# Fused four-layer kernel on one core: W's last part transposed earlier into another bank, a tanh layer's second half in quarters, two more tiles seeded by ScalarE

## The reference, cut to what matters

```python
x = x + diffusion(x, zX, zY, zR)                       # 5-point stencil with reflecting edges, + reaction term
# layer 1: scores of each row, softmax of them under a mask per row, pooling of the rows of x
attn_in = jnp.tanh(jnp.einsum('bsd,da->bsa', hidden, W1) + b1)      # W1: 512 x 128
scores = jnp.einsum('bsa,a->bs', attn_in, v)
p = jax.nn.softmax(jnp.where(mask, scores[:, None, :], NEG_INF), axis=-1)
x = x + jnp.einsum('bjl,bld->bjd', p, hidden) / cnt[..., None]
# layer 2: a 512 x 512 weight and bias chosen per batch
x = x + jnp.einsum('bnh,boh->bno', x, W) + b[:, None, :]
# layer 3: adapter 512 -> 128 -> 512, then layer norm; weights chosen per batch
z = jax.nn.relu(jnp.einsum('bsh,bhk->bsk', hidden, Wd) + bd)
y = hidden + jnp.einsum('bsk,bkh->bsh', z, Wu) + bu
x = x + (y - mu) * jax.lax.rsqrt(var + EPS) * g + b
```

## Time and profile before

| What | Value |
|---|---|
| Median of 3 runs | 583.63 us (580.74 to 593.93) |
| The profiled execution, whole | 589.26 us |
| Its span, first to last instruction | 587.4 us |
| Mean granted TensorE clock | 0.975 |
| TensorE matmul row busy | 561.6 us (96%) |
| TensorE weight loads | 440.1 us (75%) |
| VectorE | 447.8 us (76%) |
| ScalarE | 335.8 us (57%) |
| GpSimd | 291.7 us (50%) |
| DMA | 93.84 MB, mean 160 GB/s |

### The profile page before, as it was taken

How to read it: one execution, slowest core, us unless ns; L and a number is a source line. 1 busy time by engine, 2 the same in 40 slices (tenths; PEclk the granted TensorE clock), 3 DMA queues, 4 the chain that set the end, 5 groups by cost and what they waited for, 6 DMA issues and landing times.

```text
span 587.4 us, 9333 instructions
## 1 busy us (share of the span) xinstructions
PE 561.6 (96%) x2934; PEld 440.1 (75%) x2934; DVE 447.8 (76%) x1176; ACT 335.8 (57%) x587; POOL 291.7 (50%) x271
## 2 busy tenths in 40 slices
PE   8996689999999999999999999999999999999995
PEld 2356577788768887788768887788769887788784
DVE  7745778778975988778975988778976988767456
ACT  3434465466846667466846567465846568445440
POOL 6635441577328553577228553577237653326221
PEclk9696979999999999999999999999999999999999
DMA  5479008795499548994499548994599548124352
GB/s 167 138 273 162 2 1 259 238 186 103 115 302 239 110 85 229 309 199 93 122 300 236 114 89 199 335 201 82 129 278 251 118 94 196 21 72 80 76 98 88
DMA packets 60000, 93.84 MB, mean 160 GB/s; under 512 B 10999, under 2 KB 15607, under 8 KB 59952
## 3 DMA queue, kind: packets, MB, share of 16 engines
q0 software_dynamic: 16544, 29.90, 31.0%
q1 hardware_dynamic: 34192, 46.58, 24.8%
q10 hardware_dynamic: 9216, 16.78, 7.8%
HBM read 61.26 MB, written 31.98 MB: 159 GB/s over the span
## 4 chain that ended last, share of the span: by engine, by line
PE 85%; DVE 8%; issue 3%; ACT 2%; DMA 1%; POOL 0%; SPq 0%; DVEq 0%; ACTq 0%
PE y L644 34%; PE front_ps L680 9%; PE front_ps L644 8%; PE front_ps L758 6%; PE front_ps L703 5%; PE front_ps L656 4%; DVE x2f L1456 4%; PE front_ps L723 3%; PE front_ps L688 3%; PE y L813 2%; PE front_ps L694 2%; PE y L669 2%; PE y L665 2%; PE front_ps L733 1%; DVE xd L1321 1%
## 5 line engine op out<-in xcount | busy, mean ns | idle before, releaser
L534 POOL TENSOR_TENSOR norm<-norm 128x1 f32<-128x1 f32 x64 | 45.1, 704 | 134.1 <-DVE norm L1489 134.1
L644 PE MATMUL y<-wth,x2h 128*128 128x512 f32 x256 | 102.7, 401 | 0.0
L644 PE MATMUL y<-wth,x2l 128*128 128x512 f32 x256 | 100.6, 393 | 0.0
L644 PE MATMUL y<-wtl,x2h 128*128 128x512 f32 x256 | 100.0, 391 | 0.0
L541 POOL DMA_DIRECT2D out<-o_sb x58 | 64.7, 1154 | 39.2 <-ACT o_sb L1060 38.2
L1478 DVE BATCH_NORM_STATS2 stats<-y 128x6 f32<-128x512 f32 x64 | 44.4, 693 | 50.0 <-PE y L644 50.0
L510 POOL TENSOR_TENSOR xd<-xn 128x1024 f32<-128x1024 f32 x28 | 54.2, 1937 | 43.6 <-DVE x L1328 23.0
L558 POOL TENSOR_TENSOR x2l<-x2f,x2h 128x1024 fp32r<-128x1024 f32 x24 | 57.4, 2390 | 29.7 <-ACT x2h L929 29.7
L1456 DVE SCALAR_TENSOR_TENSOR x2f<-alb,small,front_ps 128x128 f32<-128x128 f32 x256 | 70.1, 340 | 1.2
L758 PEld LDWEIGHTS front_ps<-th_pt,x 128*128 128x128 f32 x512 | 62.8, 194 | 9.1 <-DVE x2f L1456 6.8
L758 PE MATMUL front_ps<-th_pt,x 128*128 128x129 f32 x512 | 65.5, 281 | 3.2 <-DVE x2f L1456 2.7
(11 more groups left out here) (149 smaller groups left out, 1176.5 us busy)
## 6 DMA issues: line engine op xcount, KB each, us to landing
xn<-in_x SPq DMA_DIRECT2D x32, 512.0 KB, 10.2
out<-x ACTq DMA_DIRECT2D x58, 256.0 KB, 4.7
out<-o_sb POOLq DMA_DIRECT2D x58, 256.0 KB, 6.2
xu<-in_x SPq DMA_DIRECT2D x21, 512.0 KB, 9.7
xu<-in_x POOLq DMA_DIRECT2D x21, 512.0 KB, 7.8
wn<-in_L_cond_weight SPq DMA_DIRECT2D x8, 1024.0 KB, 5.7
wd<-in_L_cond_down_w SPq DMA_DIRECT2D x8, 256.0 KB, 6.0
wu<-in_L_cond_up_w SPq DMA_DIRECT2D x8, 256.0 KB, 3.8
```

Source lines behind the costliest of these rows:

```text
L534: pool.tensor_tensor(rstd[:, r:r + 1], ve[:, r:r + 1], minus_half[:, :], ALU.pow).then_inc(rstd_ready, 1)
L644: ins = mm(dst, lhs, rhs, start=first and q == 0, stop=last and q == len(parts) - 1, skip_group_check=True)
```

## The change

W's last part goes to cbank, right behind adapter_down, instead of to pair_a behind spread_bias; what guards it is rest_w of part 1. The hidden layer's second half becomes two quarters: rows 512 to 767 in cbank, rows 768 to 1023 in pair_a, each with a tanh of its own. Tiles 1 and 7 join those seeded by ScalarE. ScalarE's and VectorE's orders follow.

```diff
@@ banks, constants
-        hidden_ps = (cbank, pair_a[:, 0:512])
+        HIDDEN = (slice(0, HALF), slice(HALF, HALF + 2 * P), slice(HALF + 2 * P, S))
+        hidden_ps = (cbank, cbank[:, 0:2 * P], pair_a[:, 0:2 * P])
-        w_ps = (pair_b, cbank, pair_a[:, 0:D])
+        w_ps = (pair_b, cbank, cbank)
-        SEEDED = (3, 4, 5, 6)
+        SEEDED = (1, 3, 4, 5, 6, 7)
@@ TensorE: transpose_x1, the waits for c = 0 to 3
-                wait_past(pe, *((wtl_ready, 3 * n - 2), (wtl_ready, 3 * n), (x1t_ready, NC * n + 1),
+                wait_past(pe, *((wtl_ready, 3 * n - 2), (zf_ready, 4 * n), (x1t_ready, NC * n + 1),
                                 (x1t_ready, NC * n + 2))[c])
@@ TensorE: score_hidden
-            def score_hidden(n, q, h):
-                pe.wait_ge(x1t_ready, NC * n + 2 * h + 2)
-                if h == 0:
+            def score_hidden(n, q, part):
+                pe.wait_ge(x1t_ready, NC * n + part + 2)
+                if part == 0:
                     wait_past(pe, x2s, KD * NG * n)
-                    wait_past(pe, wtl_ready, 3 * n - 1)
+                    wait_past(pe, wtl_ready, 3 * n)
+                elif part == 1:
+                    pe.wait_ge(th_ready, 3 * n + 1)
                 for k in range(KD):
-                    ins = mm(hidden_ps[h], w1[:, k, :], x1t[q][:, k, half(h)],
+                    ins = mm(hidden_ps[part], w1[:, k, :], x1t[q][:, k, HIDDEN[part]],
                              start=k == 0, stop=k == KD - 1)
@@ TensorE: spread_scores
-                pe.wait_ge(th_ready, 2 * n + h + 1)
                 pe.wait_ge(x1t_ready, NC * n + 3)
-                mm(pair_b[:, half(h)], v_col[:, 0:1].to_broadcast([P, P]), th[:, half(h)], start=True, stop=True
-                   ).then_inc(sc_ps, 1)
+                for part in ((0,), (1, 2))[h]:
+                    pe.wait_ge(th_ready, 3 * n + part + 1)
+                    ins = mm(pair_b[:, HIDDEN[part]], v_col[:, 0:1].to_broadcast([P, P]), th[:, HIDDEN[part]],
+                             start=True, stop=True)
+                ins.then_inc(sc_ps, 1)
@@ TensorE: scores_by_row, down_through_w
-                pe.wait_ge(th_ready, 2 * n + 2)
+                pe.wait_ge(th_ready, 3 * n + 3)
@@ TensorE: transpose_w
                     if hb == 3:
-                        pe.wait_ge(zf_ready, 4 * n + 4)
+                        pe.wait_ge(wtl_ready, 3 * n + 2)
@@ TensorE: linear
-                if t < 2 or t == 7:
+                if t == 0:
@@ TensorE: program, the opening
                     score_hidden(m, 1 - q, 1)
+                    score_hidden(m, 1 - q, 2)
@@ TensorE: program
                     adapter_down(n, q)
+                    transpose_w(n, 2)
...
                     spread_bias(n, q)
-                    transpose_w(n, 2)
                     linear(n, q, 0)
...
                     score_hidden(m, 1 - q, 1)
                     spread_scores(m, 0)
+                    score_hidden(m, 1 - q, 2)
                     spread_scores(m, 1)
@@ ScalarE: hidden(n, part) works on HIDDEN[part]; seed
+                act.wait_ge(bias_kept, b + 1)
                 act.wait_ge(y_free, NJ * b + before(t, YB) + 1 + CREDIT)
@@ ScalarE: program, the last tiles of the last batch
                     store_last(2)
-                    for t in range(5, NJ):
+                    keep_last_x3(5)
+                    seed(b, 7)
+                    store_last(3)
+                    for t in range(6, NJ):
@@ ScalarE: program, the opening
                     hidden(m, 1)
+                    hidden(m, 2)
@@ ScalarE: program
                     round_x2(n, q, 2)
                 if b is not None:
+                    seed(b, 7)
                     scale(b, 4)
...
                     adapter_relu(n, 0)
+                    round_w(n, 2)
                     adapter_relu(n, 1)
                     keep_x1t(m, 1 - q, 0)
-                    round_w(n, 2)
-                    scale(b, 5)
+                    keep_bias(n)
                     scale_rows(m, 3)
+                    seed(n, 1)
                     centre(m, 2)
                     keep_x1t(m, 1 - q, 1)
                     centre(m, 3)
+                    scale(b, 5)
                     scale(b, 6)
-                    keep_bias(n)
                     keep_x3(n, 0)
...
                     keep_x1t(m, 1 - q, 3)
+                    hidden(m, 1)
+                    hidden(m, 2)
                     round_up(m, 1 - q)
-                    hidden(m, 1)
@@ VectorE: program
                     diffuse(m, 1 - q, 1)
+                if n is not None:
+                    rest_w(n, 2)
                 if b is not None:
                     moments(b, 7)
                     subtract_mean(b, 1 - q, 7)
-                if n is not None:
-                    rest_w(n, 2)
```

More of the change, by code:

```diff
@@ L970, in keep_x1t, with hidden @@
                      pair[:, :].rearrange("p (k q) -> p k q", k=KD)).then_inc(x1t_ready, 1)
-            def hidden(n, h):
+            def hidden(n, part):
                 wait_past(act, p_mm, KD * n)
-                act.wait_ge(h_ps, 2 * n + h + 1)
-                act.activation(th[:, half(h)], hidden_ps[h], ACT.Tanh,
+                act.wait_ge(h_ps, 3 * n + part + 1)
+                act.activation(th[:, HIDDEN[part]], hidden_ps[part], ACT.Tanh,
                                bias=b1_col[:, 0:1]).then_inc(th_ready, 1)
@@ L1180, in program @@
                 if n is not None:
-                    round_w(n, 2)
-                if b is not None:
-                    scale(b, 5)
+                    keep_bias(n)
                 if m is not None:
                     scale_rows(m, 3)
+                if n is not None:
+                    seed(n, 1)
+                if m is not None:
                     centre(m, 2)
```

## The result

The changed kernel took 581.22 us in the median of 20 runs (576.72 to 590.15), against 585.85 us for the kernel before (20 runs, 580.74 to 594.05). The ratio is 0.9924, with a 95% interval of 0.9896 to 0.9953: faster by 0.8%, some 4.5 us, where 7.9 us (1.4%) were forecast. The time lies in the range; the gain is a little over half of the forecast, and against the 583.63 us from which the forecast started the 581.22 us are only 2.4 less.

A forecast was written before the change was run, and what follows sets the result against it. TensorE's instruction stream was taken to set the period. The terms, -5.8 - 1.3 - 1.7 + 0.8 + 1.5 - 1.4 = -7.9 us, taken from 583.63, gave 575.7 us, with a range of 570 to 584.

The forecast's parts named there:

- 1, W's last part: Transposes of W's last part no longer wait for pair_a: 0.57 us a middle batch, 5.8 us in all.
- 2, the two seeds: Linear of tiles 1 and 7 loses a bias matmul, 0.233 us each: 1.7 us for tile 1, 1.3 for tile 7.
- less 0.2: Tile 1's seed in the first batch: 0.2 us taken off the 0.233 us won in each of 8 batches.
- That is a tie: Tile 7's seed seen at 272.25, linear reaching it at 272.21: 0.15 us gained in each of 7 batches.
- 3, the quarters: Tanh layer's second half in two 256-column parts: 0.8 us added for ten more passes a batch, 1.5 for the stall.
- The stall becomes 0.24 - 0.21 + 0.43 = 0.46, so 0.22 is lost in each of 7 batches: TensorE's wait on the last tanh in spread_scores, with less cover: 1.5 us added in all.
- 4, the opening: First batch's hidden layer no longer waits whole for keep_x1t(3): 1.4 us gained, bounds 0 and 1.5.
- (a): ScalarE's queue becomes the bound at linear(n,1) through a late seed: 585.6 us, chance 0.05.
- (b): round_w(2) or rest_w(2) late for linear(n,0), or relu holds pair_a; W's 5.8 us lost: 581.5 us, chance 0.10.
- (c): The opening's low clock falls elsewhere: 572.7 or 578.7 us, chance 0.15 each.
- A steady period above 66.4 would make the prediction wrong: Sign to check in the new trace: the steady period was forecast at about 65.8 us, from 66.4.

The follow-up runs named there:

- e2: The kernel before with only the move of W's last part: median 575.98 us, ratio 0.9876.
- e1: The changed kernel with the hidden layer's second half whole again, W's move and the seeds kept: median 574.39 us, ratio 0.9847.
- e7: The e4 kernel with tile 7's seed put ahead of round_x2(n, 2) on ScalarE: ratio 0.9817.
- e3: The kernel before with only the hidden layer's second half split into quarters: ratio 0.9995.
- e4: The changed kernel with both quarters' products ahead of both spread_scores, which covers the last tanh: median 573.27 us, ratio 0.9818.
- e11: The e4 kernel, unchanged, run once more in a single execution: 582.05 us.
- e8: The changed kernel, unaltered, measured and profiled once more: ratio 0.9968 to the kernel before.
- e5: The changed kernel with quarter 1's 256-column product in spread_scores(1) made twice, filling the last tanh's stall: ratio 0.9873.
- e10: The e5 kernel, unchanged, run once more in a single execution: 574.38 us.

## Why the prediction was right or wrong

**1, W's last part: right.** Forecast 0.57 us a period; e2 against before gives 66.36 - 65.81 = 0.55. The longer waits of the first and the last batch, 1.03 and 1.37 in the forecast, are gone as well: from spread_bias to linear's bias product it is now 0.31 us in the first (76.31 to 76.62) and 0.23 in the last (542.41 to 542.64). Nothing that was moved around it came late: no wait of linear on wtl, and none on zh. The timeline of ACT agrees with the slot foreseen for round_w: behind the first half's relu, ahead of the second's.

**2, the two seeds: right in kind, one term too large.** Forecast 0.23 + 0.15 a period; e1 against e2 gives 65.81 - 65.56 = 0.25. Tile 1's seed ends in time in the full periods, with the margin of 0.3 to 0.4 us that was worked out; in the first batch it is late, as the forecast's "less 0.2" had it (linear's first product starts 0.92 us behind the transposes ahead of it, 79.62 to 80.54, where a full period has 0.78). Tile 7's does not, as these rows of the changed kernel show, first ACT:

```profile
196.31 0.58 ACT L936 ACTIVATE y<-bias_all 128x512 f32<-128x512 f32 x1
```

then PE:

```profile
196.62 0.40 PE L645 MATMUL y<-wuh,zl 128*128 128x512 f32 x1
196.94 0.50 PE L645 MATMUL y<-wth,x2h 128*128 128x512 f32 x1
197.28 0.40 PE L645 MATMUL y<-wtl,x2h 128*128 128x512 f32 x1
```

and PEld, the load of the weights of the product that waited:

```profile
196.94 0.19 PEld L645 LDWEIGHTS y<-wth,x2h 128*128 128x128 f32 x1 [0.36 <-ACT y L936]
```

The seed ends at 196.89 and linear's first product starts at 196.94 instead of 196.85 (a step of 0.23 behind the one at 196.62). The step to the next is then 0.34 and not 0.23: its weights were loaded only at 196.94, with it, where the other products here have theirs loaded one step ahead. PEld shows the same wait in all six full periods. "That is a tie" took the arrival as the whole cost; a late seed also loses the 0.1 us of overlap. Of the 0.23 only 0.23 - 0.09 - 0.11 = 0.03 was left where 0.15 was forecast, and e7 won 0.19 back by moving the seed. That is nearly all of the missing 0.13.

**3, the quarters: the step that failed.** Its plain terms were good: a stall of 0.46 was forecast and 0.45 found; 0.22 for it and 0.10 for the passes were to be added to the period, and 0.26 in all was (e1 against the changed kernel; e3 against before gives 0.24), so the passes cost next to nothing: in e4's chain of waits 16 passes of 256 columns advance by 3.45 us, where 8 of 512 take 3.43. In this the smaller fixed cost of the Trainium skill ("TensorE: Matmul & The Clock Gate", "Back-to-back issue gap"), which the prediction set beside its own, was the nearer. What failed is the sentence "The stall becomes 0.24 - 0.21 + 0.43 = 0.46, so 0.22 is lost in each of 7 batches": it priced idle time at its own length. Its real price was the clock it cost afterwards, 1.63 us for each fall, 3 to 6 times in the profiled executions, against 0.2 us for the added idle time itself. The term for the clock behind the stall was put at nothing, without a reason. No row of before showed a fall in the steady part, and I had taken that for a property of the steady part. It was one of the margin: the kernel before already had 0.24 us of stall and 1.7 us of one-column passes there.

**4, the opening: right.** The hidden layer's last eight transposes start at 29.93 and the one-column passes at 36.22, 6.29 us; before 34.78 and 42.37, 7.59. So 1.30 us was won of 1.4 forecast, with the granted clock at 1.00 in both stretches.

**The rivals.** (a) and (b) did not come; every margin they attacked held. (c) was right that the granted clock would decide, and put it in the wrong place: the opening's clock varies, by more than it said (11.4 us between e4 and e11), but with one program as well, so it is no part of the change. The falls in the steady part, which are part of it, stood in no rival. "A steady period above 66.4 would make the prediction wrong" caught it: three of the six full periods are 67.4. Here the Trainium skill's remark that the clock's window runs freely ("TensorE: Matmul & The Clock Gate", "The HAM clock gate") fits that the falls are not in the same batches in two profiles of one kernel (e8 and the first), though no run here shows the window itself. What rival (c) took from it, that the clock would then be no effect of the change, does not hold: e1, e2 and e5 show that it was one.

**The sum.** Without falls the change is worth 6 x 0.54 = 3.2 us in the steady part, 1.3 in the opening, and 1.0 and 1.4 in the waits of the first and last batch: 6.9 us, and the late seed accounts for most of what is missing to 7.9. e5, which is the change without falls, measured 0.9873, or 7.4 us of 585.85. The 3 us between that and the 4.5 measured I put down to the falls. That share is argued, not shown: the two intervals overlap, the profile has 6.5 us of falls, and how many a timed execution had can't be read. The absolute time is off by more, 581.22 against 575.7, since the forecast started from a median of three runs, 583.63, that was 2.2 us below that of twenty.

## What to carry to other kernels

Idle time on TensorE can have a second price. Here a stall of 0.45 us next to 1.7 us of one-column products made the granted clock fall in 13 of 21 periods, and the next dense block paid 1.63 us. So look behind every stall for a block that is longer in some periods than in others. When a product group is split so that its consumer starts sooner, count the cover that the last piece is left with: the same instructions in another order (e4) are 1.8% faster than before, where the change is 0.8%. Time the edits of such a change one by one, and compare steady periods, not spans.

## What the runs showed of the hardware that was not expected

- The granted clock fell from 2.4 to 1.2 GHz (1.00 to 0.50 in the windows) in a stream in which PE was busy in every slice by the page: behind a stall of 0.45 us and 16 one-column passes of 1.7 us. Filling the stall with products, at equal length, kept it up (14 of 14 periods, e5 and e10).
- A fall cost 1.63 us in each of the 13 periods (3.68 to 5.31 for 32 passes), and which periods had one varied between two executions of one kernel.
- Tile 7's product that waited for its seed lost about 0.1 us beyond the wait: the step behind it was 0.34 us instead of 0.23, and its weights were loaded with it and not ahead.
- The opening of one program took 11.4 us more in one execution (e11) than in another (e4). The stretch from 15 to 25 us was granted 0.50 in e11 and 1.00 in e4, for no cause that the kernel shows; what decides it stays open.
